# Tensor-product layer of a four-layer graph network: one-hots made on ScalarE instead of VectorE

## What is computed

```python
ys = xs @ w1_s * inv                        # 64 scalars a node
yv = einsum('nud,uv->nvd', xv, w1_v) * inv  # 64 vectors of 3 a node
h = silu(edge_attr @ fc_w1 * 8**-0.5)       # 8 numbers an edge
h = silu(h @ fc_w2 * 64**-0.5)
wA, wB, wC, wD = split(h @ fc_w3 * 64**-0.5, 4, axis=1)
es, ev = ys[dst], yv[dst]                   # gathered per edge
m0a = wA * es * sh0
m0b = wD * einsum('eud,ed->eu', ev, sh1) * 3**-0.5
m1a = wB[:, :, None] * es[:, :, None] * sh1[:, None, :]
m1b = wC[:, :, None] * ev * sh0[:, :, None]
ns = segment_sum(concat([m0a, m0b]), src)   # 512 sums a node in all
nv = segment_sum(concat([m1a, m1b]), src)
deg = segment_sum(ones, src)
```

## Time and profile before

| | us |
|---|---|
| three runs | 9693.83, 9711.04, 9713.11 |
| median of the three | 9711.04 |
| span of the profiled execution | 9714.6 |
| in it, from the first record of the layer to its last ScalarE instruction | about 1511 |
| TensorE busy, whole span | 6352.9 (65%) |
| VectorE busy, whole span | 5950.3 (61%) |
| ScalarE busy, whole span | 2466.4 (25%) |
| GpSimd busy, whole span | 5883.0 (61%) |

### The profile page before, as it was taken

The page is one execution under the profiler, slowest core; times in us unless marked ns, Lnnn a source line. Parts: engine busy times, 40 slices in busy tenths (PEclk is TensorE's granted clock), DMA queues, the critical chain, the costliest instruction groups (busy, mean ns, idle before and its releaser), DMA issues. The chain is left out here.

```text
span 9714.6 us, 128477 instructions
## 1 busy us (share of the span) xinstructions
PE 6352.9 (65%) x28538; PEld 4079.3 (42%) x28761; DVE 5950.3 (61%) x16480; ACT 2466.4 (25%) x7477; POOL 5883.0 (61%) x5564
## 2 busy tenths in 40 slices
PE   2111144444454545448999997899999997778775
PEld 0000033333333333334444444555555555666664
DVE  4100166666666666657888887899999997222224
ACT  0000033333333333322333332344444442000000
POOL 5777655555555555546777774566666665666663
PEclk6555566666666666669999998999999998888887
DMA  1000122222222222322222233344444444233334
GB/s 64 1 10 12 29 82 82 79 79 79 82 78 79 80 82 78 79 51 79 83 83 83 83 83 50 112 120 118 119 119 119 120 118 99 86 87 88 86 88 55
DMA packets 405872, 777.60 MB, mean 80 GB/s; under 512 B 195938, under 2 KB 225356, under 8 KB 405196
## 3 DMA queue, kind: packets, MB, share of 16 engines
q0 software_dynamic: 279488, 712.60, 27.9%
q1 hardware_dynamic: 126348, 64.59, 2.3%
HBM read 736.75 MB, written 40.07 MB: 80 GB/s over the span
## 5 line engine op out<-in xcount | busy, mean ns | idle before, releaser
L495 POOL DMA_INDIRECT rec_s<-wts,rows x784 | 778.3, 993 | 1187.2 <-ACT rows L467 949.9
L1845 POOL DMA_INDIRECT gat<-y,rec_sb_s x892 | 1157.9, 1298 | 343.2 <-issue 320.0
L2114 POOL DMA_INDIRECT gat<-x,rec_sb_d x892 | 844.3, 947 | 525.4 <-issue 259.9
L1397 POOL DMA_INDIRECT gat<-kv,rec_sb_s x900 | 861.7, 957 | 398.5 <-issue 314.0
L968 POOL DMA_INDIRECT gat<-kv,rec_sb_d x896 | 857.8, 957 | 318.1 <-issue 277.3
L1593 DVE TENSOR_REDUCE small<-ps 128x2 f32<-128x1024 f32 x884 | 1041.7, 1216 | 5.7 <-PE ps L1461 4.4
L434 POOL DMA_INDIRECT rec_d<-small x784 | 815.8, 1041 | 336.7 <-issue 258.9
L990 PE MATMUL ps<-work,oh 128*128 128x128 bf16 x896 | 113.0, 266 | 1323.1 <-DVE oh L1156 1245.3
L1886 PE MATMUL ps<-big,oh 128*128 128x512 f32 x1760 | 948.2, 638 | 0.0
L1001 PE MATMUL ps<-qz,work 128*128 x1792 | 769.2, 604 | 143.4 <-issue 143.4
L2151 DVE TENSOR_TENSOR acc<-acc,ps 128x256 f32 x220 | 92.2, 419 | 1020.5 <-remote 735.5
(11 more groups left out here) (281 smaller groups left out, 13973.6 us busy)
## 6 DMA issues: line engine op xcount, KB each, us to landing
gat<-kv,rec_sb_s POOLq DMA_INDIRECT x900
gat<-kv,rec_sb_d POOLq DMA_INDIRECT x896
rec_sb_s<-rec_s SPq DMA_DIRECT2D x448, 32.0 KB, 2.2
gat<-y,rec_sb_s POOLq DMA_INDIRECT x892
gat<-x,rec_sb_d POOLq DMA_INDIRECT x892
rec_d<-small POOLq DMA_INDIRECT x784
rec_s<-wts,rows POOLq DMA_INDIRECT x784
rec_s<-gat SPq DMA_DIRECT2D x4, 1808.0 KB, 17.1
```

The source lines that it names most:

```text
L495: e.indirect_dma_start(out=recs["s"], out_offset=bass.IndirectOffsetOnAxis(ap=pr[:, t:t + 1], axis=0), in_=rr[:, t, :], in_offset=None).th ...
L1397: e.indirect_dma_start(out=gat[:, m.u, q, :], out_offset=None, in_=table, in_offset=bass.IndirectOffsetOnAxis(ap=r_sb[:, m.u, q, 0:1].bitc ...
L1845: e.indirect_dma_start(out=rows_y[m.u][:, q, :], out_offset=None, in_=y1, in_offset=bass.IndirectOffsetOnAxis(ap=r_sb[:, m.u, q, 0:1].bitc ...
L2114: e.indirect_dma_start(out=gat[:, m.u, q, 0:D], out_offset=None, in_=x3, in_offset=bass.IndirectOffsetOnAxis(ap=r_sb[:, m.u, q, 0:1].bitca ...
```

## The change

VectorE makes no one-hots in this layer. ScalarE makes them in two steps. `distances` computes |node number - n| for n = 0 to 127 with four Abs activations (scale -1, the node number as bias) into a new tile `away` in an unused part of `work`. `one_hots` waits for these through the new semaphore `far`, and computes max(0, 1 - distance) for all four groups with one Relu of 512 columns, which is 1.0 at distance 0 and 0.0 at every other whole number. They are spread over `act` and made for the same macro M+2 (before: M+3, on VectorE). The first two macros' one-hots stand ahead of everything else on ScalarE.

```diff
+            def distances(e, m, some):
+                if some[0] == 0:
+                    e.wait_ge(s_rec[m.u], m.turns(16))
+                    e.wait_ge(s["oh"], m.done(1))
+                for q in some:
+                    last = A.activation(away[:, q, :], iota[:, :], ACT.Abs, scale=-1.0, bias=r_sb[:, m.u, q, 1:2])
+                if some[-1] == Q - 1:
+                    last.then_inc(s["far"], 1)
+
+            def one_hots(e, m):
+                e.wait_ge(s["far"], m.done())
+                e.wait_ge(s["sum"], m.done(U))
+                A.activation(oh[:, m.u, :, :], away, ACT.Relu, scale=-1.0, bias=1.0).then_inc(s["oh"], 1)
+
-            def act(e, m):
+            def act(e, m, nxt=None):
                 e.wait_ge(s["tr"], m.done())
                 e.wait_ge(s["h1"], m.done(1))
                 A.activation(at, ps[0:Q * WS, 0, 0:P], ACT.Copy).then_inc(s["at"], 1)
+                if nxt:
+                    distances(e, nxt, range(0, 1))
                 e.wait_ge(s["h1"], m.done())
                 e.wait_ge(s["h2"], m.done(1))
                 A.activation(h1, ps[:, 1, 0:2 * P], ACT.Silu, scale=8.0 ** -0.5).then_inc(s["g1"], 1)
+                if nxt:
+                    distances(e, nxt, range(1, 3))
                 e.wait_ge(s["h2"], m.done())
                 e.wait_ge(s["w"], m.done(1))
                 A.activation(h2, ps[:, 0, 0:2 * P], ACT.Silu, scale=MUL ** -0.5).then_inc(s["g2"], 1)
+                if nxt:
+                    distances(e, nxt, range(3, Q))
+                    one_hots(e, nxt)
...
-            def one_hot(e, m, q):
-                if q == 0:
-                    e.wait_ge(s_rec[m.u], m.turns(16))
-                    e.wait_ge(s["sum"], m.done(U))
-                ins = V.tensor_scalar(oh[:, m.u, q, :], iota[:, :], r_sb[:, m.u, q, 1:2], None, ALU.is_equal)
-                if q == Q - 1:
-                    ins.then_inc(s["oh"], 1)
...
                 k = c(V.tensor_tensor(g3, yv, shb, ALU.mult))
-                one_hot(e, nxt, 0)
-                one_hot(e, nxt, 1)
                 c.wait(k)
                 k = c(V.tensor_tensor(dot, g3[:, :, 0, :], g3[:, :, 1, :], ALU.add))
-                one_hot(e, nxt, 2)
                 c.wait(k)
                 k_dot = c(V.tensor_tensor(dot, dot, g3[:, :, 2, :], ALU.add))
-                one_hot(e, nxt, 3)
...
+            def scalar(e):
+                for m in range(2):
+                    distances(e, Macro(0, m), range(Q))
+                    one_hots(e, Macro(0, m))
+                macro_loops(2, act, lambda e, M: act(e, M(2), M(2)))(e)
```

More of the change, by code:

```diff
@@ L1796, in layer1 @@
             project("p1", 2, qz, loads, groups, evac, store_rows(y1, D), prepare=split)
-            s = stages("e1", "oh", "tr", "at", "h1", "g1", "h2", "g2", "w", "wac", "wr", "msg", "sum", "flush")
+            s = stages("e1", "far", "oh", "tr", "at", "h1", "g1", "h2", "g2", "w", "wac", "wr", "msg", "sum", "flush")
             s_rec = [sem(f"e1_rec{u}") for u in range(U)]
@@ L1810, in layer1 @@
             h2 = work[:, 384:640]
+            away = work[:, 640:1152].rearrange("p (q n) -> p q n", q=Q)
             wac = work[:, 1536:2048].rearrange("p (q a n) -> p q a n", q=Q, a=2)
@@ L1925, in act, with messages @@
                 last.then_inc(s["wac"], 1)
-            def one_hot(e, m, q):
-                if q == 0:
-                    e.wait_ge(s_rec[m.u], m.turns(16))
-                    e.wait_ge(s["sum"], m.done(U))
-                ins = V.tensor_scalar(oh[:, m.u, q, :], iota[:, :], r_sb[:, m.u, q, 1:2], None, ALU.is_equal)
-                if q == Q - 1:
-                    ins.then_inc(s["oh"], 1)
-            def messages(c, e, m, nxt):
+            def messages(c, e, m):
                 y = rows_y[m.u]
@@ L1977, in dve @@
                 e.sem_inc(S("e1_go"), 1)
-                for m in range(2):
-                    for q in range(Q):
-                        one_hot(e, Macro(0, m), q)
                 cc = Chain(e, cB)
-                messages(cc, e, Macro(0, 0), Macro(0, 2))
+                messages(cc, e, Macro(0, 0))
                 per = cc.n
@@ L1989, in turn @@
                     c.enter(M(1).i, U * per)
-                    messages(c, e, M(1), M(3))
+                    messages(c, e, M(1))
                     assert c.n - c.at == per
@@ L1998, in pool @@
                 all_landed(e, every_gather)
-            phase(sync=sync, gpsimd=pool,
-                  scalar=macro_loops(2, act, lambda e, M: act(e, M(2))), tensor=tensor, vector=dve)
+            def scalar(e):
[3 more added lines that the diff above has]
+                macro_loops(2, act, lambda e, M: act(e, M(2), M(2)))(e)
+            phase(sync=sync, gpsimd=pool, scalar=scalar, tensor=tensor, vector=dve)
             w2 = wts[:, 0:P].rearrange("p (k n) -> p k n", k=2)
```

## The result

The kernel after takes 9799.42 us (median of 4, 9796.07 to 9803.06) against 9702.44 us of the kernel before (median of 4, 9691.05 to 9713.11): ratio 1.0088, interval 1.0074 to 1.0102. It is 97 us slower. Forecast was 9703, and the range ended at 9745. The profiled execution took 9803.06 us, its span is 9801.3 us.

The account below looks back on a forecast made before the run. TensorE, in a ring with ScalarE of 6.60 us a turn, was taken as the bound. From the median 9711.0 us, 0 (turns) + 0 (start) - 8 (late ends) gave 9703; range 9685 to 9745.

Parts of the forecast that it names:

- The ring: Tensor-product layer's loop: L1875, L1924 with L1914, L1860 to L1875 bound each turn, which stays at 6.60 us.
- VectorE's one-hots are worth 0: Tensor-product loop: removing four L1931 frees VectorE 0.3 to 0.7 us a turn, off the ring; value 0.
- ScalarE's holes: ScalarE's idle times before L1917, L1920 and L1924 take the added 2.17 us a turn; value 0 while they hold.
- The rule of the Trainium skill that the prediction quotes against the change: Use VectorE, not ScalarE, for relu, max, add, mul; if the busy difference had to be paid: 222 us, 9933 us.
- The start: First two macros' one-hots move to ScalarE before its first L1914; net -0.7 to +0.5 us, taken as 0.
- Late turns: 24 of 55 loop ends came about 1 us late; change worth -24 to +33 us, taken as -8.
- GpSimd gets slack: Tensor-product loop: VectorE's two-SBUF-input operations end earlier, so somewhat fewer late loop ends; part of the reason for -8 us.
- 2 (ScalarE in the ring): Operation or wait over twice its row: 22 us for each 0.1 us over, up to 9933; chance 0.05.
- 3 (VectorE as hidden bound): VectorE's 0.7 us count in each turn: 9711 - 155 = 9556; chance 0.04.
- 1 (late at every loop end): Same ring, GpSimd settles in the bad position: +33 us, 9744; chance 0.11.
- none of the four: The three numbered rivals and a fourth: change does nothing or late ends vanish, both inside the forecast of chance 0.68.
- The rule of the Trainium skill on the port: VectorE's fp32 tensor_scalar can hold GpSimd's descriptor port; by it all late ends would go, 9687; prediction said the trace disagrees.

Follow-up runs that it names:

- s_both: Kernel after with VectorE's four one-hots a turn put back as idle work, ScalarE's new work kept, timed at the upper level: 1.0010 of the kernel before.
- e1_both: Kernel after with VectorE's one-hots put back as idle work, ScalarE's work kept; level with the kernel before at 8338 us, stretch 1438.9 us.
- e2_none: Kernel after without ScalarE's one-hot work in the loop, tiles filled once (sums wrong); level with the kernel before at 8338 us, stretch 1439.0 us.
- e3_together: Kernel after with all four Abs behind the second Silu, ahead of the Relu; level with the kernel before at 8338 us, stretch 1439.9 us.
- t_fill: Kernel after with a GpSimd memset of a spare tile behind each turn's four gathers: 9542 us, 0.9995 of the kernel before.
- t_after: Kernel after, unchanged, timed again as the measure for its series: 9627 us, 1.0075 of the kernel before.
- k_jump_fill: Kernel after with one turn in four's gathers waiting for ScalarE's first Silu, plus a GpSimd memset behind each turn's gathers: 0.9977 of the kernel before.
- t_half: Kernel after with two of a turn's four gathers left out (messages wrong), at the upper level; the ring runs at its 1440 us.
- j_jump: Kernel after with one turn in four's gathers waiting for ScalarE's first Silu, at the upper level: 1.0821 of the kernel before.
- i_jump: Kernel after with one turn in four's gathers waiting for ScalarE's first Silu, at the lower level: level with the kernel before at 8343 us.

## Why the prediction was wrong, point by point

- The ring (TensorE L1875, ScalarE L1924 and L1914, TensorE again) and its 6.60 us: right. The median turn after is 6.606 us.
- VectorE's one-hots are worth 0: right for the ring by their time, and incomplete: VectorE's wait at L1979 is 1.27 us at 4833.83 instead of 0.71, 0.56 longer, within the 0.3 to 0.7 forecast. But they kept GpSimd's gathers at 1.3 us, and so at a steady pace. The prediction put no price on that; s_both shows that it was worth nearly the whole loss (1.0010, interval 0.9998 to 1.0022).
- ScalarE's holes: right. Idle before L1934 0.51 (forecast 0.5), before L1939 0.55 (forecast 0.5); the Abs 394 ns (385), the Relu 630 (630); busy up by 405 us over the span (forecast 420), VectorE down by 140 (forecast 250, from a count of busy time that overlaps between neighbours: the page counts less). TensorE's waits for the two Silus stand only in long turns. At the lower level e1_both, e2_none and e3_together confirm it. The rule of the Trainium skill that the prediction quotes against the change (VectorE and not ScalarE for such operations) would have been right on the result and, with s_both at 1.0010, wrong on the reason.
- The start: right in sum. The first four turns are disturbed in both kernels, 41.1 us from the first copy to the fourth scalings before and 43.2 after.
- Late turns, valued at -8 us with ends at -24 and +33: this is the step that failed. On the known events the direction was right: the 1 us late loop ends are down from 24 to 2. But the sentence "GpSimd gets slack" was taken for a gain. The slack made the gathers catch up after each stumble, and the term measures +85 us: +105.5 us of long turns (109.8 against 4.3) and -20.2 us of late loop ends (2.4 against 22.5). The 1 us and the new 5 us look alike: in the kernel before the signal of L1875 itself stands 0.93 to 1.02 us late 24 times, and never at the lower level (e1_both). That both have one cause is likely but was not tested.
- The ends of that term were set by how often the known 1 us could occur, 0 or 55 times. Nothing bounded how large such an event can be, though the trace of before had larger ones at its start. The timeline of the kernel before has, ahead of its steady stretch,

```profile
4455.23 0.38 ACT L1917 ACTIVATE work<-ps 128x256 f32<-128x256 f32 x1 [4.88 <-remote]
...
4463.17 1.14 ACT L1924 ACTIVATE work<-ps,rec_sb_s 128x128 f32<-128x128 f32 x4 [6.32 <-remote]
```

The first of these rows, 4.1 us more than the usual 0.80, is an event of the same size as the later ones. It was the nearest to a bound, and it was left out. At 22 such events of 5 us the range would have reached past 9799; that there would be 22 of them, no row of before could tell.
- The rivals: 2 (ScalarE in the ring) and 3 (VectorE as hidden bound) are refuted by e1_both, e2_none and the turn of 6.606 us. 1 (late at every loop end) didn't happen. What did happen was none of the four.
- The rule of the Trainium skill on the port (that fp32 tensor_scalar can hold it, and tensor_tensor, as inferred, does not) fares as in the prediction: with no one-hot left on VectorE there are still gathers of 1.40 and 1.59 us, as at 4828.34 and 4825.19, started inside tensor_tensor operations. Yet the mean fell from 1298 to 1019 ns, so the one-hots did slow the gathers; by which way was not tested.

## What to carry to other kernels

Work taken off an engine that waits can still change the result through the engines that it slows: ask which of them gets slack, what it will do with that slack, and whether it will run in bursts instead of at a pace. Here a stream of gathers that can run ahead and must catch up was worse than one that is steadily behind, and an idle operation of 0.44 us that fills GpSimd's turn was worth 84 us (t_fill 9542 us, t_after 9627). Where a trace holds events that no view explains, bound the term that hangs on them by the largest such event seen anywhere in it, not by the usual one. Time at more than one occasion, since at one of the levels seen here the effect is absent. And before a run is taken as a test, look in its trace whether the edit did what it was for: in k_jump_fill it did not.

No version with right results clearly beats the kernel before. k_jump_fill, 0.9977 (0.9961 to 0.9993) at 9699 us, is the nearest; t_fill, which does nearly the same, has 0.9995, and neither was timed at 8340 us.

## What the runs showed of the hardware

- While GpSimd issued gathers in fast unbroken runs (one in 1.3 to 1.4 us), TensorE's completion signals stood up to 13 us late in the traces, at the upper level only; no recorded signal of ScalarE or VectorE did. A run of 16 gathers in 20 us cost 13.0 us. In runs of up to 95 gathers at one in 1.65 us the steady turns were at most 1 us late.
- The kernel before ran at about 8340 or at 9500 to 9750 us by the series. In this layer a record lands 1.7 to 1.8 us after its load at both levels (1.77 us in t_half at the upper, 1.81 in e3_together at the lower).
- In the kernel after GpSimd stops once in 104 gathers, for 1.6 to 2.1 us instead of 0.30 between two gathers, at the same gathers in each of its three traces; with half of the gathers (t_half) once in 108. In j_jump and i_jump there is no such stop, and in e1_both a gather of 2.6 us stands in its place.
- A gather that starts inside one of VectorE's operations with two SBUF inputs ended 0.82 to 0.89 us behind that operation's end (378 of them in the kernel after): 4828.34, inside the L1957 of 4827.96, took 1.40 us, and an undisturbed one takes 0.95.
